# A DRAM scratch reordered from (tile, time, channel) to (block, time, tile, channel) between a convolution and an MLP

## The reference, cut to what matters

```
x1  = x  + 0.5 * (fft_ffn(LN(x)))                       # a 512 x 512 matrix and a bias
z   = LN(x1)
y   = s4d(LN'(z))            # a causal convolution over time, per channel, its kernel a sum of 64 decays
xm  = z + y ;  g = LN(xm)
x2  = x1 + xm + fc2(gelu(fc1(g)))                       # fc1: 512 -> 2048, fc2: 2048 -> 512
out = x2 + 0.5 * (fft_ffn(LN(x2)))
```

## Time and profile before

| what | value |
|---|---|
| median of three runs | 2135.66 us (2135.25 to 2138.02) |
| the profiled execution | 2134.51 us, its span 2132.7 us |
| granted TensorE clock, mean | 0.973 |
| TensorE busy | 1962.6 us, 92% of the span |
| VectorE busy | 1247.5 us, 58% |
| ScalarE busy | 748.5 us, 35% |
| DMA queue of SP | 231460 packets, 189.47 MB |
| convolution stage | from about 414 to 600 us |
| MLP stage | from 622 us to the end |

### The profile page before, as it was taken

One profiled execution on the slowest core, in us unless ns is written; L12 is line 12 of the kernel. 1 busy time (PEld: TensorE's weight loads), 2 busy tenths in 40 slices (PEclk: granted clock), 3 DMA queues, 4 the chain that ended last, 5 costly groups with the idle time before them and its releaser, 6 DMA issues.

```text
span 2132.7 us, 27911 instructions
## 1 busy us (share of the span) xinstructions
PE 1962.6 (92%) x10107; PEld 963.3 (45%) x10128; DVE 1247.5 (58%) x2099; ACT 748.5 (35%) x1003; POOL 537.7 (25%) x415
## 2 busy tenths in 40 slices
PE   7975777499859999999999999999999999999997
PEld 6432333277634444444444444444444444444443
DVE  4876999778964728264462826446282644628242
ACT  1365777765632404122240412224041222404111
POOL 0165777655421202111120211112021111202101
PEclk8997999799979999999999999999999999999999
DMA  7144332269972122221212223121222312122011
GB/s 247 79 173 162 119 118 99 89 191 308 278 224 40 40 60 60 65 74 41 60 40 60 60 65 74 41 60 40 60 60 65 74 41 60 40 60 60 25 35 40
DMA packets 231575, 191.14 MB, mean 90 GB/s; under 512 B 142754, under 2 KB 177186, under 8 KB 230691
## 3 DMA queue, kind: packets, MB, share of 16 engines
q1 hardware_dynamic: 231460, 189.47, 30.7%
HBM read 100.82 MB, written 63.41 MB: 77 GB/s over the span
## 4 chain that ended last, share of the span: by engine, by line
PE 79%; DVE 8%; DMA 5%; issue 4%; ACT 2%; SPq 1%; POOL 0%; ACTq 0%; DVEq 0%; POOLq 0%; another core or an unknown queue 0%
PE psum L1555 31%; PE psum L1572 31%; PE psum L1459 9%; DMA arena<-in_x 3%; PE psum L1510 2%; PE psum L1501 1%; PE psum L1422 1%; DVE arena L1136 1%; DVE bn L969 1%; DVE bn L1144 1%; DVE ring L1192 1%; DVE taps L1092 1%; PE psum L1519 1%; PE psum L1433 1%; PE psum L1440 1%
## 5 line engine op out<-in xcount | busy, mean ns | idle before, releaser
L1555 PE MATMUL psum<-arena 128*128 128x512 f16 x3072 | 667.2, 380 | 24.4 <-DMA arena<-taps 23.3
L1572 PE MATMUL psum<-arena 128*128 128x512 f16 x3072 | 665.7, 379 | 0.0
L849 ACT ACTIVATE arena<-psum,b1p,sc 128x512 f32<-128x512 f32 x256 | 199.2, 778 | 1059.4 <-PE psum L1555 1058.4
L1555 PEld LDWEIGHTS psum<-arena 128*128 128x128 f16 x3072 | 300.5, 98 | 389.3 <-issue 29.1
L1572 PEld LDWEIGHTS psum<-arena 128*128 128x128 f16 x3072 | 300.6, 98 | 362.5
L577 POOL TENSOR_TENSOR va<-va,mhalf 128x4 f32<-128x4 f32 x80 | 91.2, 1144 | 1245.4 <-DVE va L962 1222.8
L1376 DVE SCALAR_TENSOR_TENSOR arena<-psum,sc,arena 128x512 f32<-128x512 f32 x64 | 48.0, 751 | 578.7 <-PE psum L1572 578.7
L1352 DVE SCALAR_TENSOR_TENSOR arena<-arena,sc 128x512 f16<-128x512 f32 x256 | 244.0, 953 | 9.1
L1459 PE MATMUL psum<-m_parts,taps 128*128 128x512 f16 x768 | 184.5, 392 | 68.8 <-DVE taps L1092 68.7
L1459 PE MATMUL psum<-m_parts,arena 128*128 128x512 f16 x768 | 169.8, 381 | 10.2 <-DMA arena<-taps 10.2
L1349 DVE TENSOR_SCALAR arena<-arena,sc 128x512 f16<-128x512 f32 x256 | 137.4, 537 | 50.1 <-ACT arena L849 49.9
(11 more groups left out here) (159 smaller groups left out, 1766.0 us busy)
## 6 DMA issues: line engine op xcount, KB each, us to landing
arena<-in_x SPq DMA_DIRECT2D x16, 1024.0 KB, 9.9
x_scratch<-arena SPq DMA_DIRECT2D x16, 1024.0 KB, 4.3
taps<-taps_copies SPq DMA_DIRECT2D x64, 256.0 KB, 4.3
y_scratch<-arena SPq DMA_DIRECT2D x32, 512.0 KB, 6.0
arena<-y_scratch SPq DMA_DIRECT2D x15, 1024.0 KB, 7.1
arena<-x_scratch SPq DMA_DIRECT2D x15, 1024.0 KB, 5.5
out<-arena SPq DMA_DIRECT2D x15, 1024.0 KB, 4.9
taps<-taps_copies SPq DMA_DIRECT2D x64, 128.0 KB, 4.8
```

The costliest lines, as they stand in the source:

```text
L849: act.activation(h32[:, hc % 4, :], bank(hc % 2), ACT.Gelu, scale=scale(C_W1), bias=b1p[:, hc:hc + 1])\
L1555: last = pe.matmul(bank(hc % 2), w1_sb[:, a, k, hc * P:(hc + 1) * P], gt[:, b, k, :], start=(n == 0), stop=(n == 3 * KC - 1))
L1572: last = pe.matmul(bank(4 + j % 2), hid[:, a, hc, j * P:(j + 1) * P], w2_sb[:, b, hc, :], start=(n == 0), stop=(n == 3 * HC - 1))
```

## The change

`y_scratch` was (64 tiles, 128 rows, 512 channels); it becomes (4 blocks, 128 rows, 64 tiles, 128 channels). A store of an eighth of a block is eight tiles of 128 channels on each partition. Before, each of these eight pieces of 512 bytes went to another place in DRAM; now the eight lie behind each other in DRAM as they do in the stage, 8 x 512 = 4096 bytes a partition and store (the whole run of a block and row is 32 KB). The loads are changed to fit: a group's y is, for each block and row, four tiles of 128 channels, 2048 bytes; before it was, for each tile and row, 512 channels, 2048 bytes. For group 0, where a load takes one tile and three blocks, a piece was 1536 bytes and is 512 bytes.

The MLP's on-chip buffer of y (`ybuf`, groups 1 to 15) is ordered (block, tile, channel) instead of (tile, channel). Each VectorE and ScalarE instruction that reads or writes a tile of it therefore has four runs of 128 elements, 2048 bytes apart, in its access pattern, and its other operands are viewed in the same way. The buffer of group 0 (`first_y`) is written as (tile, block, channel), which is the same place for each element as before. Nothing is computed differently, and the order of the instructions on each engine is the same.

```diff
-    y_dram = nc.dram_tensor("y_scratch", (TILES, P, C), F32, kind="Internal").ap()
+    y_dram = nc.dram_tensor("y_scratch", (BLOCKS, P, TILES, BLK), F32, kind="Internal").ap()
...
-        ybuf = buffer(at4 + size)
-
-        first_y, first_x1 = buffer(2 * REG), buffer(2 * REG + size)
+        ybuf = area(at4 + size, size).rearrange("p (b j c) -> p j b c", b=BLOCKS, j=GT)
+
+        first_y = area(2 * REG, size).rearrange("p (j b c) -> p j b c", b=BLOCKS, j=GT)
+        first_x1 = buffer(2 * REG + size)
...
+        def by_block(ap):
+            return ap.rearrange("p (b c) -> p b c", b=BLOCKS)
+
+        def z2_by_block(j, part):
+            return by_block(z2_parts[:, j, part, :])
...
-                sp.dma_start(y_dram[at, :, blk * BLK:(blk + 1) * BLK].rearrange("t p c -> p t c"),
-                             stage[:, at, :]).then_inc(y_stored[blk][i if blk < 2 else 0], 16)
+                sp.dma_start(y_dram[blk, :, at, :], stage[:, at, :]).then_inc(y_stored[blk][i if blk < 2 else 0], 16)
...
-                sp.dma_start(first_y[:, j, 0:C - BLK], y_dram[j, :, 0:C - BLK]).then_inc(first_loaded[j], 16)
+                sp.dma_start(first_y[:, j, 0:BLOCKS - 1, :], y_dram[0:BLOCKS - 1, :, j, :].rearrange("b p c -> p b c"))\
+                  .then_inc(first_loaded[j], 16)
...
-                sp.dma_start(ybuf, y_dram[bass.ds(g * GT, GT), :, :].rearrange("j p c -> p j c"))\
+                sp.dma_start(ybuf.rearrange("p j b c -> p b j c"),
+                             y_dram[:, :, bass.ds(g * GT, GT), :].rearrange("b p j c -> p b j c"))\
                   .then_inc(yg_loaded, 16)
...
-                    dve.scalar_tensor_tensor(out=y[:, j, :], in0=rbuf[par][:, j, :],
-                                             scalar=alpha1[:, bass.ds(4 * g + j, 1)], in1=y[:, j, :],
+                    dve.scalar_tensor_tensor(out=y[:, j, :, :], in0=by_block(rbuf[par][:, j, :]),
+                                             scalar=alpha1[:, bass.ds(4 * g + j, 1)], in1=y[:, j, :, :],
                                              op0=ALU.mult, op1=ALU.add).then_inc(xm_sum, 1)
                 dve.wait_ge(xm_sum, 4 * g + j + 1)
-                ins = dve.bn_stats(bn[:, 0, j, :], y[:, j, :])
+                ins = dve.bn_stats(bn[:, 0, j, :], y[:, j, :, :])
```

More of the change, by code:

```diff
@@ L823, in z2 @@
                     act.wait_ge(gt_turned[j], 16 * g)
-                act.activation(z2_parts[:, j, 0, :], y[:, j, :], ACT.Identity,
+                act.activation(z2_by_block(j, 0), y[:, j, :, :], ACT.Identity,
                                scale=va[:, 1, j:j + 1], bias=va[:, 2, j:j + 1]).then_inc(z2_high, 1)
                 act.wait_ge(z2_high, 4 * g + j + 1)
-                act.activation(y[:, j, :], y[:, j, :], ACT.Identity,
+                act.activation(y[:, j, :, :], y[:, j, :, :], ACT.Identity,
                                scale=va[:, 1, j:j + 1], bias=va[:, 2, j:j + 1]).then_inc(z2_ready, 1)
@@ L1272, in mixed @@
                     last = slice(C - BLK, C)
-                    dve.scalar_tensor_tensor(out=y[:, j, last], in0=first_x1[:, j, last], scalar=alpha1[:, j:j + 1],
+                    dve.scalar_tensor_tensor(out=y[:, j, BLOCKS - 1, :], in0=first_x1[:, j, last], scalar=alpha1[:, j:j + 1],
                                              in1=area((BLOCKS - 1) * REG + j * BLK, BLK), op0=ALU.mult,
@@ L1299, in residual @@
                 y, x1 = (first_y, first_x1) if is_first(g) else (ybuf, rbuf[par])
-                dve.scalar_tensor_tensor(out=rbuf[par][:, j, :], in0=y[:, j, :],
-                                         scalar=beta1[:, bass.ds(4 * g + j, 1)], in1=x1[:, j, :],
+                dve.scalar_tensor_tensor(out=by_block(rbuf[par][:, j, :]), in0=y[:, j, :, :],
+                                         scalar=beta1[:, bass.ds(4 * g + j, 1)], in1=by_block(x1[:, j, :]),
                                          op0=ALU.add, op1=ALU.add).then_inc(r_sum, 1)
@@ L1307, in z2_split @@
                 dve.wait_ge(z2_ready, 4 * g + j + 1)
-                dve.tensor_tensor(z2_parts[:, j, 1, :], y[:, j, :], z2_parts[:, j, 0, :], ALU.subtract)\
+                dve.tensor_tensor(z2_by_block(j, 1), y[:, j, :, :], z2_by_block(j, 0), ALU.subtract)\
                    .then_inc(z2_low, 1)
@@ L1330, in _ @@
                 dve.wait_ge(first_loaded[j], 32)
-                dve.scalar_tensor_tensor(out=first_y[:, j, 0:C - BLK], in0=first_x1[:, j, 0:C - BLK],
-                                         scalar=alpha1[:, j:j + 1], in1=first_y[:, j, 0:C - BLK],
+                rest = first_x1[:, j, 0:C - BLK].rearrange("p (b c) -> p b c", c=BLK)
+                dve.scalar_tensor_tensor(out=first_y[:, j, 0:BLOCKS - 1, :], in0=rest,
+                                         scalar=alpha1[:, j:j + 1], in1=first_y[:, j, 0:BLOCKS - 1, :],
                                          op0=ALU.mult, op1=ALU.add).then_inc(first_mixed, 1)
```

## The result

The changed kernel takes 2133.16 us (median of 20 runs) beside 2136.97 us for the kernel before (20 runs): ratio 0.9981, 95% interval 0.9974 to 0.9988, which is 2.6 to 5.6 us faster. Taken again later it is 0.9987 (0.9978 to 0.9996). The forecast was 6.9 us less, 2128.8 us, in a range from 2125.5 to 2135 us. The measured time lies in this range, but only in the part that was taken in for the rivals: the range of the forecast itself ended at 2131.2 us. Of the 4.4 us between 2128.8 and 2133.16 us, 1.3 us come from the base, since the median of 20 runs of the kernel before is 1.3 us above that of the three which the forecast started from. So the sign holds, and the gain is about half of the forecast.

A forecast was written before the change was run, and what follows sets the result against it. TensorE was taken to bound the kernel, busy 92%, with three transfer waits outside the MLP's main work. Savings of 3.0 + 2.8 + 1.1 = 6.9 us gave 2128.8 us, range 2125.5 to 2135.

The forecast's parts named there:

- The stores: Stores of y in 4096-byte instead of 512-byte pieces: each takes 0.5 us less DMA time, bounds 0 to 0.62.
- The first place: Convolution, o = 27 to 29, TensorE waiting for late taps: 3.0 us less, bounds 0 and 3.65.
- with 0.5 us less a store it grows by 0.36: Transfer backlog at o = 24 to 28: growth for each o falls from 0.86 to 0.36 us.
- SP's holding: SP held up issuing the weight load (2.29 us) and tap loads behind a store (1.98 us, where 1.2 would do).
- The second place: Convolution, o = 42 to 45, VectorE waiting for the maxima's store and load: 2.8 us less, bounds 0 and 3.7.
- With 3.5 to 4 us to land: Store of the maxima: lands in 3.5 to 4 us after the change, 6.29 before.
- 0 if these small transfers keep their latency: Lower bound at o = 42 to 45: no gain if the maxima's store and load take as long as before.
- The third place: Way into the MLP, L1273 waiting for the first y loads: 1.1 us less, bounds 1.9 less and 2 more.
- Costed at nothing: Last eight stores, covered by transposes, and MLP instructions on the reordered `ybuf`, covered by TensorE: 0 us.
- slower: Rival: pieces 32 KB apart meet in the same part of DRAM and slow the stores; 2161 us, chance 0.08.
- One place only: Rival: the maxima's round trip is latency, or late weights remain at o = 27 to 29; 2132.5 us, chance 0.14.

The follow-up runs named there:

- strided23: Changed kernel, but stores of blocks 2 and 3 take every eighth tile, so pieces of 512 bytes in the new layout; 2134.37 us, ratio 0.9984 to the kernel before.
- short0: Changed kernel, but each of block 0's eight stores takes one tile instead of eight, the rest of its place filled in the FFN stage; 2127.28 us (1 run).
- x1early: Changed kernel with group 0's four x1 loads issued inside the loop at o = 61 and 63, not at its end; 2133.30 us, ratio 0.9983 to the kernel before.

## Why the prediction was right, and where it was off

**The stores** were sized well: 0.5 us less for each, bounds 0 to 0.62, and 0.56 measured where they are alone in the queues (406 GB/s). `strided23` shows that this comes with the size of a piece.

**The first place, 3.0 us, is the term that was mis-sized.** The step that failed is "with 0.5 us less a store it grows by 0.36": it takes the saving of a store alone for a saving in the mix. Over the burst the mix moved 339 to 341 GB/s before and 348 to 364 after: the 1179 KB of a value of o take 3.46 us and then 3.24 to 3.39, so 0.07 to 0.22 us less, not 0.5. With the stores of block 0 an eighth as long the place is gone (`short0`), so bytes set it; with the same bytes in an eighth as many packets it stays for the most part. Measured 4.2 to 2.5 in the mean of two profiles each, 1.7 us; over the five profiles with these stores it is 1.0, inside the scatter. SP's holding I read as a cost; it was for the most part only where the queue stood. With the weight load issued in 0.48 us the tap load itself took 9.62 us.

**The second place, 2.8 us, gave 1.6** (1.4 over the five profiles). That SP gets to the store of the maxima earlier was right (523.29, 1.2 us behind the end of `between(38)`, where 1.3 was forecast and 3.7 was before), and that VectorE sets the pace from the scales on too: from the scales to the last `stage_y` it is 63.45 us before and 63.49 after. "With 3.5 to 4 us to land" was wrong: 7.2 to 8.8 us in all profiles with the 4 KB stores, of which about 5 are there where only taps are queued. The bound "0 if these small transfers keep their latency" was wrong too: the store's latency did not fall at all, it rose, and the place still gave something, because SP came to it 3 us earlier.

**The third place, 1.1 us, gave nothing** (1.7 before, 2.1 after). The forecast took 1.5 us off for a smaller backlog of block 2's stores, and no row stood behind that number. The last load of y lands 64.7 and 64.2 us behind the start of the scales before, 65.3 and 64.4 after: no sooner. What holds it stays open, since `x1early` doesn't settle it. Whether the pieces of 512 bytes in the loads themselves cost part of it was not tried.

**Costed at nothing, and right:** the MLP stage has the same TensorE time, and the instructions on the new `ybuf` the same length, `z2`'s 802 ns as in the earlier trace rows. From L1273 to fc1 it takes 20.2 and 20.6 us before, 20.4 in both profiles after, though the last store lands at 611 and not at 617: they were covered, as said.

The sum of the places is 1.7 + 1.6 - 0.4 = 2.9 us, the medians say 3.8 and 2.9. That the two agree so well is in part luck, since each place scatters by 1 us from profile to profile. It is luck too, and not the working, that brings the time into the stated range: it was widened for the rivals. The rival *slower* is refuted by `strided23` and the 406 GB/s. *One place only* came nearest in its number (2132.5 us) and was half right in its reason: the maxima's time to land didn't fall and the first place kept late taps, but no place came whole, and two of them became smaller. What stays open is what limits the mix of loads and stores to 339 to 364 GB/s, when fc1's long store moves 393 and the stores of y 406 alone.

## What to carry to other kernels

Larger pieces speed up a transfer that has the queues to itself; where loads and stores already overlap and the queues are full, look first at whether the total rate rises with the piece at all (here 2 to 7%, not 43%); fewer bytes in that stretch helped where larger pieces alone did little. When a queue holds up its issuer and the holding goes away, look for the same time in the landing of what comes next. And where several consumers sit behind one queue (taps, weights, a small round trip), moving bytes away from one puts them in front of the next; take the whole chain as the measure, not the place. A place that becomes shorter can do so because its start moved: look at when the awaited transfer lands.

## What the runs showed of the hardware

- Stores to DRAM alone in the queues: 283 to 293 GB/s with pieces of 512 bytes in either layout, 406 GB/s with pieces of 4096 bytes, 32 KB from row to row. The mix with tap and weight loads: 339 to 341 and 348 to 364 GB/s. The Trainium skill, DMA: Bandwidth & Descriptors (Specifications), gives 512 bytes as the least transfer at line rate. These runs don't agree: by their rows a store at 512 bytes reaches 0.7 of the rate at 4 KB.
- A store of 1 KB in 128 pieces of 8 bytes took 4.6 and 5.3 us to land at a share of 0.6 to 0.7, of which 2.5 and 3.7 us came after its last packet; a store of 64 KB in 128 pieces of 512 bytes took 3.8 us, 0.7 of it after the last packet. Tap loads around the first narrow store landed after 3.7 to 6.6 us, without it after 3.1 to 3.4.
- The start of the convolution alone, before any edit, scattered from 419.1 to 424.3 us over profiles in which the same instructions came before it.
